# Reordering the start of an adaptive-layer-norm MoE kernel: sigmoid first, first norm on two engines, products of ones on TensorE

## The reference

```python
mod = (_silu(L0_c) @ L0_wmod).reshape(L0_c.shape[0], 6, 1, -1)     # c: 4 x 256, wmod: 256 x 1536
sa, ca, ga, sb, cb, gb = (mod[:, 0], mod[:, 1], mod[:, 2], mod[:, 3], mod[:, 4], mod[:, 5])
...
h = _layernorm(x, axis=-1) * (1 + ca) + sa                          # x: 4 x 512 x 256, float32
x = x + ga * _L0_attn_ref(h, wq, wk, wv, wo)                        # 16 heads of 16, softmax over 512 keys
h = _layernorm(x, axis=-1) * (1 + cb) + sb
x = x + gb * _L0_ffn_ref(h, ...)                                    # 32 experts, top 4, and a shared expert
```

## Time and profile before

| | us |
|---|---|
| median of 3 runs | 596.38 |
| lowest and highest of them | 596.19, 599.55 |
| the profiled execution's own time | 599.47 |
| its span, core 0 | 597.7 |
| PE busy in that span | 560.9 |

### The profile page before, as it was taken

How to read it: one execution, slowest core, us unless ns; L and a number is a source line. 1 busy time by engine, 2 the same in 40 slices (tenths; PEclk the granted TensorE clock), 3 DMA queues, 4 the chain that set the end, 5 groups by cost and what they waited for, 6 DMA issues and landing times.

```text
span 597.7 us, 10693 instructions
## 1 busy us (share of the span) xinstructions
PE 560.9 (94%) x3102; PEld 308.7 (52%) x3103; DVE 374.9 (63%) x888; ACT 255.3 (43%) x519; POOL 206.1 (34%) x268
## 2 busy tenths in 40 slices
PE   4989999999999999999999998989998999999983
PEld 3443323233333333333343455638887898988572
DVE  6375577778679786798856469545343443442588
ACT  3112635664866648555568240123333343444000
POOL 6200000000020751207533663722665666667200
PEclk9975999999999999999999999999999999999998
DMA  6133117100221222212100688433544655540592
GB/s 228 40 110 123 27 34 218 34 7 16 68 49 37 80 82 77 44 35 82 62 1 29 222 255 249 136 91 107 157 146 137 180 161 159 166 125 18 209 404 91
DMA packets 44119, 67.18 MB, mean 112 GB/s; under 512 B 9499, under 2 KB 32420, under 8 KB 43692
## 3 DMA queue, kind: packets, MB, share of 16 engines
q1 hardware_dynamic: 31984, 45.62, 26.5%
q0 software_dynamic: 7680, 16.87, 8.1%
q10 hardware_dynamic: 4416, 4.20, 2.1%
HBM read 38.93 MB, written 27.51 MB: 111 GB/s over the span
## 4 chain that ended last, share of the span: by engine, by line
PE 83%; DVE 9%; DMA 2%; issue 2%; SPq 2%; ACT 1%; POOL 0%; ACTq 0%; DVEq 0%; POOLq 0%
PE ps L875 23%; PE ps L888 11%; PE ps L1106 9%; PE ps L972 8%; PE ps L1127 6%; PE ps L824 5%; PE ps L966 4%; PE ps L1092 3%; PE ps L846 3%; PE ps L833 3%; PE ps L901 3%; DVE max_q L1217 2%; PE ps L1117 2%; PE ps L810 2%; PE ps L931 1%
## 5 line engine op out<-in xcount | busy, mean ns | idle before, releaser
L1217 DVE TENSOR_REDUCE max_q<-ps 128x1 f32<-128x512 f32 x256 | 163.7, 684 | 73.6 <-PE ps L846 71.7
L703 ACT ACTIVATE probs<-ps 128x512 f32<-128x512 f32 x256 | 138.0, 596 | 102.1 <-PE ps L875 101.8
L846 PE MATMUL ps<-k_rows,q_rows 31*128 31x512 f32 x512 | 150.1, 681 | 1.1 <-DMA k_rows<-qk_raw 1.1
L875 PE MATMUL ps<-q_rows,k_rows 32*128 32x512 f32 x512 | 146.4, 650 | 0.9 <-DVE max_q L1217 0.9
L561 POOL DMA_INDIRECT results<-y_sb,dest x96 | 94.9, 988 | 70.3 <-ACT y_sb L752 35.2
L875 PEld LDWEIGHTS ps<-q_rows,k_rows 32*128 32x128 f32 x512 | 41.8, 186 | 70.6 <-ACT probs L703 51.1
L1106 PE MATMUL ps<-up_sb,oT 128*128 x384 | 70.8, 327 | 0.9 <-issue 0.7
L888 PE MATMUL ps<-probs,v_ext 128*32 128x512 f32 x512 | 68.2, 605 | 1.1 <-ACT probs L703 1.1
L1106 PEld LDWEIGHTS ps<-up_sb,oT 128*128 128x128 f32 x384 | 61.3, 190 | 1.9 <-issue 1.8
L1579 DVE COPY oT<-ps 128x512 f32<-128x512 f32 x48 | 33.1, 691 | 32.8 <-PE ps L1092 32.8
L1127 PE MATMUL ps<-down_sb,e_hidT 96*128 x192 | 49.8, 382 | 4.0 <-ACT e_hidT L760 4.0
(11 more groups left out here) (181 smaller groups left out, 681.9 us busy)
## 6 DMA issues: line engine op xcount, KB each, us to landing
xe<-dispatched SPq DMA_DIRECT2D x96, 129.0 KB, 2.1
comb<-results SPq DMA_DIRECT2D x16, 512.0 KB, 10.6
up_sb<-in_up SPq DMA_DIRECT2D x12, 512.0 KB, 4.7
dispatched<-pad_rows SPq DMA_DIRECT2D x33, 129.0 KB, 4.0
down_sb<-in_down SPq DMA_DIRECT2D x4, 768.0 KB, 6.7
x<-in_x ACTq DMA_DIRECT2D x4, 512.0 KB, 4.8
q_rows<-qk_raw SPq DMA_DIRECT2D x64, 32.0 KB, 1.9
k_rows<-qk_raw SPq DMA_DIRECT2D x64, 32.0 KB, 1.9
```

Of the source, the lines that this page charges most:

```text
L703: act.activation(probs[:, u % 8, :], ps[:, st_bank(t.b, g, u), :], ACT.Exp).then_inc(exp_done, 1)
L846: pe.matmul(ps[:, banks[u % len(banks)], :], q_rows[32 * i:32 * i + ONE, b % 2, g, qt * P:(qt + 1) * P], k_rows[32 * i:32 * i + ONE, b % 2 ...
L875: pe.matmul(ps[:, st_bank(b, g, n), :], k_rows[32 * i:32 * i + 32, b % 2, g, kt * P:(kt + 1) * P], q_rows[32 * i:32 * i + 32, b % 2, g, :] ...
L1217: dve.tensor_reduce(max_q[:, g % 2, qt, i:i + 1], ps[:, banks[(16 * g + n) % len(banks)], :], AXX, ALU.max).then_inc(max_done, 1)
```

## The change

Seven edits at the start:

- `cT` has a semaphore of its own, `c_ld`; ACT's Exp waits for it and not for `wmod` as well, and so ACT's three loads of `x` behind the Exp are issued sooner as well.
- On DVE the sigmoid's three steps stand ahead of the statistics of batch 0.
- DVE clears one half of `q_rows`, POOL the other, behind its small constants.
- ACT normalises tiles 0 and 1, DVE tiles 2 and 3, with `tensor_scalar` and two scalars per token.
- ACT evicts TP0 into `hT`, DVE evicts TP1, behind the modulation columns.
- POOL clears `ones` first, and PE multiplies `ones` by `ones` 12 times ahead of the modulation product. It writes to a bank that is used later only.
- Two more such products stand between the turning of the tiles and the projections.

```diff
@@ SP, POOL, ACT
-            sp.dma_start(cT[:, :]...).then_inc(mod_ld, 16)
+            sp.dma_start(cT[:, :]...).then_inc(c_ld, 16)
...
-            sp.wait_ge(q_clear, 1)
+            sp.wait_ge(q_clear, 2)
...
+            pool.memset(ones[:, :], 1.0).then_inc(ones_s, 1)
             st.did(pool.memset(ident[:, :], 0.0))
-            st.did(pool.memset(ones[:, :], 1.0))
...
             pool.sem_inc(consts, 1)
+            pool.memset(q_rows[:, 1, :, :], 0.0).then_inc(q_clear, 1)
...
-            act.wait_ge(mod_ld, 32)
+            act.wait_ge(c_ld, 16)
             act.activation(ctmp[:, :], cT[:, :], ACT.Exp, scale=-1.0).then_inc(c_exp, 1)
...
             act.wait_ge(nmr_s, 1)
-            normalise(lead)
+            normalise(lead, range(2))
             act.wait_ge(modT_s, 1)
-            for k in range(KD):
-                to_hT(lead, f"TP{k}", 0)
+            to_hT(lead, "TP0", 0)
@@ PE
-            pe.wait_ge(mod_ld, 32)
+            def of_ones(times):
+                for n in range(times):
+                    pe.matmul(ps[:, O, 0:P], ones[:, :], ones[:, :], start=True, stop=True)
+
+            pe.wait_ge(ones_s, 1)
+            of_ones(12)
+            pe.wait_ge(mod_ld, 16)
             pe.wait_ge(c_ready, 1)
...
             for k in range(KD):
                 tokens_to_columns(lead, f"TP{k}", 0)
+            of_ones(2)
             pe.wait_ge(qkv_ld, 48)
@@ DVE
-            dve.memset(q_rows[:, :, :, :], 0.0).then_inc(q_clear, 1)
-            statistics(0, TJ)
-
+            dve.memset(q_rows[:, 0, :, :], 0.0).then_inc(q_clear, 1)
             dve.wait_ge(c_exp, 1)
             st.then(dve.tensor_scalar(ctmp[:, :], ctmp[:, :], 1.0, None, ALU.add))
             st.then(dve.reciprocal(ctmp[:, :], ctmp[:, :]))
+            dve.wait_ge(c_ld, 16)
             dve.tensor_tensor(cT[:, :], cT[:, :], ctmp[:, :], ALU.mult).then_inc(c_ready, 1)
+            statistics(0, TJ)
             minus_mean_over_deviation(0, TJ, 1)
+            dve.wait_ge(nmr_s, 1)
+            for j in (2, 3):
+                dve.tensor_scalar(xn[:, j, :], x[:, j * D:(j + 1) * D], rstd[:, j:j + 1], nmr[:, j:j + 1], ALU.mult, ALU.add).then_inc(xn_ready, 1)
             dve.wait_ge(modT_ps, 1)
...
+            frees(dve.tensor_scalar(hT[:, 1, :], full(dve, lead, "TP1"), modT[:, (2 + 1) * B:(2 + 1) * B + 1], modT[:, B:B + 1], ALU.mult, ALU.add),
+                  lead, "TP1")
```

More of the change, by code:

```diff
@@ L250, in adaln_moe_kernel @@
         modd = nc.dram_tensor("modulation", [B, 4, D], F32, kind="Internal").ap()
+        c_ld, ones_s = sem("c_ld"), sem("ones_s")
         mod_ld, qkv_ld, w_ld, sh_ld = (sem(n) for n in ("mod_ld", "qkv_ld", "w_ld", "sh_ld"))
@@ L343, in _ @@
         def _(sp):
-            sp.dma_start(cT[:, :].rearrange("p (k b) -> p k b", k=KD), c_in.rearrange("(k p) b -> p k b", p=P)).then_inc(mod_ld, 16)
+            sp.dma_start(cT[:, :].rearrange("p (k b) -> p k b", k=KD), c_in.rearrange("(k p) b -> p k b", p=P)).then_inc(c_ld, 16)
             sp.dma_start(wmod[:, :, 0:2 * D], wmod_in[:, 0:2 * D].rearrange("(k p) n -> p k n", p=P)).then_inc(mod_ld, 16)
@@ L1206, in _ @@
             st.then(dve.reciprocal(ctmp[:, :], ctmp[:, :]))
+            dve.wait_ge(c_ld, 16)
             dve.tensor_tensor(cT[:, :], cT[:, :], ctmp[:, :], ALU.mult).then_inc(c_ready, 1)
+            statistics(0, TJ)
             minus_mean_over_deviation(0, TJ, 1)
+            dve.wait_ge(nmr_s, 1)
+            for j in (2, 3):
+                dve.tensor_scalar(xn[:, j, :], x[:, j * D:(j + 1) * D], rstd[:, j:j + 1], nmr[:, j:j + 1], ALU.mult, ALU.add).then_inc(xn_ready, 1)
             dve.wait_ge(modT_ps, 1)
-            st.then(dve.tensor_copy(modT[:, 0:KD * B], ps[:, 0, 0:KD * B]))
-            dve.tensor_scalar(modT[:, KD * B:], ps[:, 0, KD * B:2 * KD * B], 1.0, None, ALU.add).then_inc(modT_s, 1)
+            st.did(dve.tensor_copy(modT[:, 0:KD * B], ps[:, 0, 0:KD * B]))
+            st.then(dve.tensor_scalar(modT[:, KD * B:], ps[:, 0, KD * B:2 * KD * B], 1.0, None, ALU.add))
+            dve.sem_inc(modT_s, 1)
+            frees(dve.tensor_scalar(hT[:, 1, :], full(dve, lead, "TP1"), modT[:, (2 + 1) * B:(2 + 1) * B + 1], modT[:, B:B + 1], ALU.mult, ALU.add),
+                  lead, "TP1")
             def score_max(b, g, n, banks=SC):
```

## The result

| | kernel before | kernel after |
|---|---|---|
| median of 20 runs each, us | 597.2 | 601.0 |
| lowest and highest, us | 594.05, 601.37 | 597.9, 602.29 |
| the profiled execution's own time, us | 599.47 | 600.50 |

The ratio of the times is 1.0046, with a 95% interval of 1.0027 to 1.0065: about 2.7 us of 597.2, less than half a per cent, but the interval lies above 1.

A forecast was written before the change was run, and what follows sets the result against it. Prediction: a stream of PE matmuls behind a start that is a relay with no engine full. Projections +4.9 us less 0.7 for the clock made +4.2 on the median 596.38, so 600.6 us, range 594.0 to 603.8.

The forecast's parts named there:

- S0: Start of the first score, 25.26 us in the kernel before; forecast 4.2 us later in the likeliest case.
- DVE held through both clearings: First norm: DVE's two tensor_scalar wait for POOL's clearings of v_ext and k_rows; projections 4.9 us later.
- The step most in doubt: First norm on DVE: an instruction held by POOL's indirect DMA is also held by a POOL memset.
- Rival A: First norm: DVE gets its turn after the first clearing, tiles at 12.9, S0 +1.0, 597.4 us; chance 0.22.
- The tiles at 16.1: First norm: DVE's normalised tiles ready at 15.8 + 0.3 = 16.1, where all were ready at 10.80 before.
- the sigmoid's steps on DVE must wait: Start, on DVE: sigmoid waits for the half clearing of q_rows, statistics start at 5.5 and not 5.20.
- The modulation product: PE, before the transposes: sigmoid's move ends it 1.0 us sooner; the products of ones give back most of that.
- The clock term: Projections on PE: products of ones raise the clock sooner, 0.7 us taken of a possible 3.0.
- S0 follows the projections: First score: SP is free by then, so projections 4.9 us later move it by +4.9.
- Rival C: PE's gap ahead of the scores grows, clock falls: up to 5.5 us more; chance alone 0.10, on likeliest case 0.12.
- the likeliest case: Start: DVE held through both clearings, +4.9 less 0.7 for the clock, 600.6 us; chance 0.42.
- Rival B: First norm: DVE isn't held, S0 gains 1.0 to 2.3 us, time 594.8 us; chance 0.20.

The follow-up runs named there:

- with POOL idle: Kernel after, with POOL's clearings of v_ext and k_rows started only when all four tiles are normalised: 598.45 us, 1.0011 of before.
- pause of 0.06 us: Kernel after, with POOL's second clearing (k_rows) waiting for completion of its first (v_ext): 600.87 us, 1.0051 of before.
- the eight caught executions: Profiled executions of eight of the twelve kernels with the half clearing of q_rows, sigmoid's step held by it; statistics start at 5.45 to 5.47.
- DVE's share without the ones: Kernel before with one edit: tiles 2 and 3 of the first norm on DVE by tensor_scalar; 1.0086 of before.
- the other form: Kernel after with DVE's two normalisations as scalar_tensor_tensor, nmr broadcast along the row, instead of tensor_scalar: 596.36 us, 0.9972 of before.

## Why the prediction was right

**The forecast** of 600.6 stands against a median of 601.0. The case was the right one. That the number fits to 0.4 us is in part luck: I put S0 2.0 us too late (4.2 against 2.15) and left out the 0.7 us that came behind it, so that the first turn starts 2.86 us later and the change cost 2.7 us by the ratio, where I had 4.2; and the median of before is 0.8 us higher over these runs, which made up for part of that.

**DVE held through both clearings: right in what it costs**, and shown from four sides: 7.08 us in the kernel after, 0.73 with POOL idle, 0.88 in another form beside the same clearing, and the whole loss from this edit alone. The step most in doubt, that an instruction held by an indirect DMA is held by a memset too, holds. How the two tiles were held is the second of the two ways that the prediction left open ("if it gets no turn between the clearings, or if only the first of the two gets one"): the first tile was ready at 11.37, and only the second went through the second clearing. The rule of the Trainium skill ("SBUF — State Buffer", section "Who interferes with whom") gave the right case. It says that whoever issues first has the ports for the whole instruction, and the trace agrees: the first tile, which was waiting, came ahead of POOL's second clearing, which then took 3.65 us instead of 3.51, and the second tile, started at 11.30, stood behind that clearing, started at 11.17. Rival A (DVE gets its turn after the first clearing) is thus true of one tile and not of the other, as its own "the second tile can lose where the first wins" had it. Its price, tiles at 12.9, is refuted, with a pause of 0.06 us too, because PE waits for all four tiles.

**The tiles at 16.1: 14.97** in the kernel after, but 16.05 in the same kernel with the pause of 0.06 us. The difference is the second hold. I let the statistics start at 5.5, because "the sigmoid's steps on DVE must wait" for the half clearing, and that is what the eight caught executions show. The one on which the profile of after rests had escaped it by 0.2 us (3.08 against 3.27). So the step was right as a common case, and the trace of after alone would have spoken against it.

**The modulation product: right as a nothing.** It ended at 7.85 instead of 11.21, more than the 1.0 us forecast: the ones were done at 5.70 and not at 7.2 to 7.6, and the product took 1.95 us where it had taken 3.55, since the clock had risen by then. All of the gain was waiting time in the end.

**The clock term: mis-sized.** I had "0.7 of the possible 3.0". The two products of ones behind the transposes carried PE to the projections without a pause, nearly all of these ran at the upper level, and they took 2.9 us less. What counted on S0 was 1.9 us, since the chain leaves PE behind the first four records and goes by SP's line. The bound was in the text: "even 3.0 would count for no more than 2.3". DVE's share without the ones has these four records at 3.71 us against 2.03, with the transposes as late, so the two products are the likely cause; they alone were not tried.

**S0 "+4.2": +2.15**, by the terms above: 4.07 - 1.92. The step that "S0 follows the projections" does not hold as it stands: from the first eviction on, SP's eight issues in a row, 20.85 to 25.34, set S0.

**Rival C came on top of the likeliest case, in part.** PE's wait ahead of S0 grew from 1.07 to 2.07 us and the clock fell, for 1.6 us more to the end of the maxima, of up to 5.5 allowed. I had given it 0.12 of the 0.42 and put nothing for it into the sum; it happened in four of the other executions too. The 0.89 us that came back in the next pause were not forecast.

**Rival B, the change as meant**, is what the other form gives (0.9972 on the first chip, that is -1.7 us): the forecast for it was 594.8, or -1.6. The number fits, the working only in part. S0 came 2.2 us sooner, at the upper end of the 1.0 to 2.3 forecast, and then rival C took most of it back, so that the first turn started 0.7 us sooner; that is B with C on top, for which I had -2 to +3.5.

## What to carry to other kernels

Before work goes from one engine to a neighbour that looks free, ask what a third engine is doing at that moment: 0.7 us of DVE work became 7.1 beside two clearings that had nothing to do with it. Where such a clearing can't be moved, another form of the instruction ran beside it at 0.44 us a tile. Where a line of a profile merges several held instructions, read them one by one: that shows whether one of them got through. A stage that is followed by a line of small transfers gives back only a part of what its own end comes sooner; the idle time that it leaves can cost the clock.

The kernel with the lowest ratios of this study is the changed one with scalar_tensor_tensor and without the products of ones: 0.9914 and 0.9928 of the kernel before, both intervals below 1, measured on the slower chips alone. That leaving out the ones is what helps is not shown. It still has the half clearing of q_rows on POOL in the sigmoid's way; to leave it on DVE was not tried.

## What the hardware showed unexpectedly

- Two waiting tensor_scalar on DVE and two clearings on POOL take turns: clearing, tile, clearing, tile, with 3.48 and 3.67 us for tiles that take 0.41 each with POOL idle, the same in each of three kernels, one of them with a pause of 0.06 us between the clearings. The clearing in the middle grew from 3.51 to 3.65 us. Even an eight-column tensor_scalar is held for all the rest of a clearing, 1.70 us instead of 0.17.
- The clock's fall in a pause isn't decided by the pause's length alone. PE's wait ahead of the first score was 2.07 us with a fall in the kernel after, and 2.07, 2.04, 1.95 and 1.95 us without one in four others.
- Where SP's small transfers come right behind the 64 KB copy of the row of ones, SP is through with the second of them only 2.99 to 3.00 us after it began to issue that copy, in five kernels, and 2.93 us in the two in which the copy was moved.
- With products on all 128 rows between the scores the granted clock stayed at 0.50 from 42 to 77 us with PE busy throughout.
- The same kernel takes 597 us on one chip and 647 to 652 on two others. Their profiles differ from the turns on, and this wasn't followed further.
